# One attention block on one Trainium2 core: another order of a piece's results, exponentials and PV on three engines

## The reference, cut to what matters

```python
# x: (1, 2048, 512); 16 heads, rank 128, rope 64, everything in float32
xn = layernorm(x)
q = (xn @ wq.T).reshape(B, S, 16, 192); q_nope, q_pe = q[..., :128], rope(q[..., 128:])
kv = xn @ wkv_a.T; kv_cache = rmsnorm(kv[..., :128], kv_norm_w); k_pe = rope(kv[..., 128:])
q_lat = einsum('bshd,hdc->bshc', q_nope, wkv_b[:, :128])
scores = (einsum('bshc,btc->bsht', q_lat, kv_cache) + einsum('bshr,btr->bsht', q_pe, k_pe)) * SCALE
attn = softmax(where(causal, scores, -1e30))
out = einsum('bshc,hdc->bshd', einsum('bsht,btc->bshc', attn, kv_cache), wkv_b[:, 128:])
x = x + out.reshape(B, S, 2048) @ wo.T + xn @ ternary(w_ffn).T + bias
```

## Time and profile before

| | |
|---|---|
| three runs | 2119.6, 2119.89, 2128.14 us; median 2119.89 us |
| the profiled execution | 2115.17 us, span 2113.1 us |
| busy share of the span | PE 85%, PE weight loads 72%, VectorE 57%, GpSimd 48%, ScalarE 40% |
| granted TensorE clock over the span | 0.92 |

### The profile page before, as it was taken

One profiled execution on the slowest core, in us unless ns is written; L12 is line 12 of the kernel. 1 busy time (PEld: TensorE's weight loads), 2 busy tenths in 40 slices (PEclk: granted clock), 3 DMA queues, 4 the chain that ended last, 5 costly groups with the idle time before them and its releaser, 6 DMA issues.

```text
span 2113.1 us, 28101 instructions
## 1 busy us (share of the span) xinstructions
PE 1803.1 (85%) x9326; PEld 1523.3 (72%) x9326; DVE 1208.9 (57%) x2801; ACT 853.5 (40%) x1358; POOL 1004.4 (48%) x635
## 2 busy tenths in 40 slices
PE   6997888778989979889888898788898888888885
PEld 5786666657777767777777777677677777777775
DVE  5764566646666655656465555455555555555552
ACT  4552443433444433344444434243443434334342
POOL 4763444434554554454444545344444544445443
PEclk9888899989999999999999999898999989999998
DMA  6992555547656565654444535546455455453544
GB/s 226 356 315 100 147 141 157 162 133 186 169 151 161 148 190 138 168 134 116 119 125 121 136 102 132 158 98 174 112 121 125 104 128 123 114 131 95 127 105 102
DMA packets 127183, 309.11 MB, mean 146 GB/s; under 512 B 29442, under 2 KB 41987, under 8 KB 125508
## 3 DMA queue, kind: packets, MB, share of 16 engines
q1 hardware_dynamic: 117152, 273.20, 48.6%
q10 hardware_dynamic: 9892, 34.18, 5.5%
HBM read 113.28 MB, written 34.60 MB: 70 GB/s over the span
## 4 chain that ended last, share of the span: by engine, by line
PE 28%; issue 20%; POOL 13%; SPq 12%; ACT 8%; DMA 5%; DVE 5%; POOLq 0%; ACTq 0%; DVEq 0%
SPq L986 11%; PE p_score L1101 10%; PE p_out L1121 9%; POOL pT L1367 7%; DMA pT<-turned 5%; PE p_result L1133 4%; DVE turned L1192 3%; ACT pT_h L1286 3%; PE p_lat L1081 3%; ACT probs L1275 3%; POOL qp_l L1356 3%; POOL qp_l L1359 3%; PE p_rot L1081 2%; ACT qp_h L1310 2%; DVE probs L1170 1%
## 5 line engine op out<-in xcount | busy, mean ns | idle before, releaser
L1367 POOL TENSOR_TENSOR pT<-pT,pT_h 128x1024 fp32r<-128x1024 f32 x320 | 684.1, 2164 | 576.4 <-ACT pT_h L1286 574.3
L1170 DVE TENSOR_SCALAR_CACHE_REDUCE probs<-p_score 128x512 f32<-128x512 f32 (+3 forms) x640 | 382.8, 602 | 617.7 <-PE p_score L1101 435.3
L1121 PE MATMUL p_out<-pT_h,V_h 128*128 128x256 f32 (+3 forms) x1024 | 327.9, 320 | 198.0 <-DVE o_l L1219 103.4
L1286 ACT ACTIVATE pT_h<-pT 128x1024 fp32r<-128x1024 f32 x320 | 291.4, 963 | 451.7 <-DMA pT<-turned 296.1
L1275 ACT ACTIVATE probs<-probs,neg_max 128x128 f32<-128x128 f32 (+15 forms) x256 | 307.0, 1199 | 378.9 <-DVE neg_max L1176 376.8
L1121 PEld LDWEIGHTS p_out<-pT_h,V_h 128*128 128x128 f32 x1024 | 213.2, 208 | 235.3 <-DVE o_l L1219 116.1
L1192 DVE STREAM_TRANSPOSE turned<-probs 128x1024 f32<-128x1024 f32 (+7 forms) x384 | 341.5, 915 | 28.2 <-ACT probs L1275 23.4
L1121 PE MATMUL p_out<-pT,V_h 128*128 128x256 f32 (+3 forms) x1024 | 323.0, 315 | 0.0
L1121 PE MATMUL p_out<-pT_h,V_l 128*128 128x256 f32 (+3 forms) x1024 | 321.8, 314 | 0.0
L1101 PE MATMUL p_score<-Kn_h,q_h 128*128 128x512 f32 (+3 forms) x640 | 249.4, 390 | 18.0 <-DVE q_l L1215 18.0
L1101 PE MATMUL p_score<-Kp,qp_h 128*128 128x512 f32 (+3 forms) x640 | 242.6, 379 | 21.3 <-POOL qp_l L1359 20.5
(11 more groups left out here) (135 smaller groups left out, 2390.0 us busy)
## 6 DMA issues: line engine op xcount, KB each, us to landing
pT<-turned SPq DMA_DIRECT2D x512, 128.0 KB, 2.3
Wq<-wq_scr ACTq DMA_DIRECT2D x63, 512.0 KB, 4.5
Wv<-wv_scr SPq DMA_DIRECT2D x63, 512.0 KB, 3.6
pT<-turned SPq DMA_DIRECT2D x256, 112.0 KB, 2.3
pT<-turned SPq DMA_DIRECT2D x256, 96.0 KB, 2.2
pT<-turned SPq DMA_DIRECT2D x256, 80.0 KB, 2.1
pT<-turned SPq DMA_DIRECT2D x256, 64.0 KB, 2.5
Wp<-wp_scr SPq DMA_DIRECT2D x31, 512.0 KB, 4.3
```

Of the source, the lines that this page charges most:

```text
L1121: mm = pe.matmul(out[:, :, cols, :], v[:, t, :], pt[:, :, t - first, rest, :], start=(t == 0 and a == 0), stop=(t == piece_tiles(s) - 1 an ...
L1170: dve.tensor_scalar(probs[row % ROW_RING][:, b * CW:b * CW + width], p_score[n % SCORE_RING][:, 0:width], SCALE, LOWEST, ALU.mult, ALU.max ...
L1286: act.activation(high.rearrange("p r t i q -> p r t (i q)"), low.bitcast(F32).rearrange("p r t i q -> p r t (i q)"), ACT.Copy).then_inc(p_ ...
L1367: pool.tensor_tensor(low.rearrange("p r t i q -> p r t (i q)"), low.bitcast(F32).rearrange("p r t i q -> p r t (i q)"), high.bitcast(F32). ...
```

## The change

Nothing is computed otherwise, and no buffer or instruction is added or removed. Seven things stand elsewhere in the engines' lists:

1. ScalarE: in chunk 3 the three first high copies of a piece move from ahead of the last exponential of slot s + 1 to the start of slot s + 2, behind it (`high_place`); in chunks 0 and 2 they move from unit 0 to unit 1. Within a unit, exponentials now come ahead of the copies of the query and the rotary part.
2. TensorE: PV runs in units 3, 4, 5 and 6 of a slot of chunk 3 (before 1, 3, 5, 7) and in 3, 4, 5 of chunk 2 (before 2, 3, 4) (`value_unit`).
3. The split of PV's result moves in chunk 3 from unit 0 of slot s + 3 to unit 7 of slot s + 2, and in chunk 2 from unit 5 of slot s + 2 to unit 0 of slot s + 3 (`split_place`, which follows `value_unit`).
4. VectorE transposes the last row of the piece before at unit 0, not 1, of each slot from 17 on.
5. The results of an earlier head go in chunk 3 to units 0, 1, 2, 2 (before 2, 3, 4, 5) (`out_unit`).
6. The query projections of chunk 3 begin a unit earlier; in chunks 0 and 3 the query's split is one unit earlier.
7. The rotary part moves: in chunk 0 TensorE makes it ahead of the slot's scores and VectorE does all five rotations at unit 0; in chunk 3 it is one unit later.

```diff
 def value_unit(s, k):
-    return (2 + k, 1 + k, 2 + k, 1 + 2 * k)[phase(s)]
+    return (2 + k, 1 + k, 6 - groups_of(s - 2) + k, 3 + k)[phase(s)]
@@ high_place
     if k < HIGH_RING:
-        return (s + 2, 0) if phase(s + 1) in (0, 2) else (s + 1, units_of(s + 1) - 1)
+        return (s + 1, units_of(s + 1) - 1) if phase(s + 1) == 1 else (s + 2, 0 if phase(s + 1) == 3 else 1)
     return s + 2, value_unit(s + 2, k - HIGH_RING)
@@ out_unit
-    return 2 + i if s % 2 == 0 else i
+    return 0 if s % 2 else (2 + i if phase(s) == 2 else (0, 1, 2, 2)[i])
@@ latent_unit
-    return (it if phase(s) == 2 else 1 + it) if s < SLOTS and closes_head(s) else None
+    return it if s < SLOTS and closes_head(s) else None
@@ query_unit
     if s < 2 * H:
-        return (3, 6)[phase(s)]
-    return (4 if phase(s) == 2 else 5) if s < SLOTS and closes_head(s) else None
+        return (2, 6)[phase(s)]
+    return 4 if s < SLOTS and closes_head(s) else None
 
 def rotate_ops(s, u):
     if phase(s) == 0:
-        return ((), (0, 1, 2), (3, 4), ())[u]
-    return ((0,), (1, 2), (3, 4))[u - 1] if 1 <= u <= 3 else ()
+        return range(5) if u == 0 else ()
+    first = rotary_unit(s) + 1
+    return ((0,), (1, 2), (3, 4))[u - first] if first <= u <= first + 2 else ()
+
+def rotary_unit(s):
+    return 1 if phase(s) == 3 else 0
 
 def rotary_add_unit(s):
-    return (2 if phase(s) == 0 else 4) if opens_head(s) else None
+    return (1, 4, 4, 5)[phase(s)] if opens_head(s) else None
 
 def rotary_high_unit(s):
-    return (3 if phase(s) == 0 else 5) if opens_head(s) else None
+    return (2, 5, 5, 6)[phase(s)] if opens_head(s) else None
@@ TensorE's slot
                 for u in range(units_of(s)):
+                    rotary = u == rotary_unit(s) and opens_head(s) and g % 2 and g + 1 < HEADS
+                    if rotary and s < H:
+                        project_rotary(g + 1)
                     if s < SLOTS:
                         scores(g, unit_of_head(s, u))
-                    if u == 0 and opens_head(s) and g % 2 and g + 1 < HEADS:
+                    if rotary and s >= H:
                         project_rotary(g + 1)
@@ VectorE's slot
-                    if 1 <= s <= SLOTS and u == (1 if s > H else 0):
+                    if 1 <= s <= SLOTS and u == 0:
                         turn_row(head_of(s - 1), first_row(s - 1) + rows_of(s - 1) - 1)
@@ ScalarE's slot
-                    if u == query_unit(s) and g + 1 < HEADS:
-                        high_query(g + 1)
-                        if g + 2 < HEADS:
-                            load_q(g + 2)
                     for old in (s - 3, s - 2):
...
                             if (s, u) == high_place(old, k):
                                 high_group(old, k)
+                    if s < SLOTS and (u + 1) % (chunk_of(g) + 1) == 0 and u + 1 < units_of(s):
+                        exp_row(g, first_row(s) + u // (chunk_of(g) + 1))
+                    if u == query_unit(s) and g + 1 < HEADS:
+                        high_query(g + 1)
+                        if g + 2 < HEADS:
+                            load_q(g + 2)
                     if u == rotary_high_unit(s) and g + 1 < HEADS:
                         high_rotary(g + 1)
-                    if s < SLOTS and (u + 1) % (chunk_of(g) + 1) == 0:
-                        exp_row(g, first_row(s) + u // (chunk_of(g) + 1))
+                if s < SLOTS:
+                    exp_row(g, first_row(s) + rows_of(s) - 1)
```

## The result

| | before | after |
|---|---|---|
| median of four runs | 2119.97 us (2119.6 to 2128.14) | 1905.83 us (1902.1 to 1907.81) |
| profiled execution, its span | 2115.17, 2113.1 us | 1902.1, 1900.0 us |
| granted clock over the span | 0.92 | 0.968 |
| ratio of after to before | | 0.898, 95% 0.8954 to 0.9005 |

The account below looks back on a forecast made before the run. A cycle of exchange, copies, exponential and transposition, not TensorE's work, was taken to pace chunk 3. Gains 95 + 66 + 12 + 21 + 5 - 8 = 191 us gave 1924, and 1929 for the median; forecast 1893 to 1970, range 1885 to 2010.

Parts of the forecast that it names:

- The ring: Chunk 3: exchange, copies, exponential and transposition wait on each other in a cycle of 22.0 us a slot, setting the pace.
- The exchange term: Chunk 3: one exchange takes 13.7 us from its start to its copies, of which 10.07 is issuing.
- The work floor: Chunk 3: TensorE's work at full clock is 70.6 us of the 89.2 us that slots 80 to 83 take.
- Chunk 3: 95 forecast: A four-slot period falls from 89.2 to 75.6 us, 3.4 a slot; 99 over 29 regular slots, taken as 95.
- the 3.0 of new waits: Chunk 3: results waiting for the split and additions add 2.5 us in an even slot, 0.5 with the rotary projection.
- Chunk 2: 66 forecast: Four slots fall from 68.9 to 59.2 us, 2.4 a slot; 68 over 28 slots, taken as 66.
- term for the six slots around the chunk changes, 12 us: The six slots around the chunk changes gain about 2 us each, 12 in all.
- Chunk 1: 21 forecast: An earlier transposition shortens PV's waits in seven slots: 15 us of idle time and 6 of clock gained.
- Chunk 0: 8 lost forecast: The third result waits about 3.4 us in every second slot; idle time even, clock drops in seven slots lose 8 us.
- exchanges slow down in denser traffic: Rival: the same DMAs packed into less time slow the exchanges; 1995 us, up to 2015 with clock falls; chance 0.17.
- The bound of 1995 us: Exchanges 1.9 us later throughout: chunk 2 pays 53 us, chunk 1 pays 13, chunk 3's cover takes it.
- The rival that short waits keep the clock down: Chunks 2 and 3: new waits of 0.5 to 1.2 us hold the clock low, losing 79 us; 2008 us; chance 0.08.

## Why the prediction was right, point by point

- **What bounds chunk 3: right, but one of two bounds.** The ring was taken as 22.0 us a slot from the earlier trace rows. With the copies put back a slot takes 21.0 us and the copies wait for exchanges again. What the prediction did not price is the second bound, PV's early place. With the exchange out of the ring but PV early, a slot still takes 21.4 us in the kernel before and 22.0 in the changed one. The prediction counted both moves as parts of the change, so its sum did not need this.
- **The exchange term: right for the kernel before.** It was sized by one exchange, 13.7 us. From the first issue to the last landing in the trace, the 26 exchanges of pieces 68 to 93 took 11.7 to 15.6 us there, 13.6 on average; with the copies put back and with only PV moved the average is 13.2. The expectation for PV alone kept 13.7, which is about half of its miss of 0.9 us a slot (21.3 for 20.4). Why the average is 0.4 us shorter is open; single exchanges in one profile differ by ten times as much.
- **The work floor: right.** 70.6 us were worked out for a period of four slots; the sum of the four above has PE busy 71.11 at full clock. Before, it was 77.06, so the lower clock cost 5.95 us of busy time, where the guess that three quarters of it were worked gave 6.5.
- **Chunk 3: 95 forecast, 113.5 measured.** The failing terms are the two added on top, "0.9 (in half of the 2.5-us slots the clock falls)" and "1.1 for uneven landings", and half of the 3.0 of new waits. The regular slots run at 1.00, the cover takes uneven landings whole, and the waits are 0.96 + 0.31 and not 2.5 (the 0.5 for `o_l` did not come) and 0.11 and not 0.5. That makes 72.6 for the 75.6, 0.75 a slot, 22 us over 29 slots. Slot 68's wait for the residual and its clock, not foreseen, take some 4 to 5 of it back.
- **Chunk 2: 66 forecast, 80.3 measured.** The wait of results on `o_l` was 1.2 (1.6), in one slot of four as said; again neither a clock drop nor a PV stall came. The period of slots 46 to 49 (1008.0 to 1064.6 us) is 56.6, from 59.2 forecast and 68.9 before; at 3.1 a slot that would be 86 over 28 slots. The **term for the six slots around the chunk changes, 12 us, was wrong**: the results' wait for the residual costs 3.5 us in slot 36 too (none before), and the wait at the end of each chunk stays. It is TensorE's rotary projection for the next chunk waiting for that chunk's `xT`, whose load is issued at 1236.03 and lands 12.3 us later; the projection starts at 1248.40. It is 12.9 us in slot 62 of the changed kernel, where before the projection waited 7.8 us and the PV after it 4.6:

```profile
PE p_rot L1086 <- issue: 12.9, 1, 12.9
```

- **Chunk 1: 21 forecast, 10.9 measured.** The PV stalls fell from 23.2 us in seven to 4.9 in three, more than said, and busy time by 6.4 us for the 6 of clock. What the step left out is an order that the diff shows: exponentials now stand ahead of the rotary copies on ScalarE, so the additions come later and almost every slot has 0.7 to 0.9 us of waiting for `acc`, 13.6 us for 0.5 before. Moving that one copy back removes these waits, which shows the cause; it returned 6 us and not 13, since PV stalls took its place.
- **Chunk 0: 8 lost forecast, 2.7 gained.** The wait on `acc` is there, 3.0 us in every second slot for 3.4. The scores' wait for the rotary low half fell in return, from 19.3 to 15.6 us, and that for the query's low half from 18.0 to 2.5, so idle time stayed about even, as forecast (53.7 and 52.2 us). The clock drop that was to follow in seven slots came in three; in the kernel with late results, whose chunk 0 is the same code, it came in six and the chunk took 265.3 us. So the 2.7 us are not clear of the spread.
- **End: 5 forecast, 5.8 measured.**
- **The sum: its small miss is partly luck.** Chunks 2 and 3 with the chunk changes were forecast at 173 us and gave 193.8, chunk 0 gave 10.7 more than forecast, chunk 1 gave 10.1 less. The last two nearly cancel, and the 12 us for the chunk changes, which did not come, hid more than half of the padding.
- **The rivals.** That exchanges slow down in denser traffic did not happen. The DMA share rose from 0.50 to 0.60, and by the trace the exchanges took 13.4 us on average in chunk 3 (13.6 before) and 12.4 in chunk 2 (13.0 before; pieces 38 to 60). One of chunk 2, 13.7 us from its start to its copies:

```profile
1011.93 4.95 SPq L991 DMA_DIRECT2D pT<-turned  x8
...
1017.60 4.96 SPq L991 DMA_DIRECT2D pT<-turned  x8
...
1025.59 2.96 ACT L1294 ACTIVATE pT_h<-pT 128x1024 fp32r<-128x1024 f32 x3 [0.69 <-DMA pT<-turned]
```

  The Trainium skill's rule that DMAs from all issuing engines share the 16 DMA engines (DMA: Bandwidth & Descriptors, Issuing engines are not separate DMA queues) asked for caution here; at a share of 0.60 the averages show no cost of it. The bound of 1995 us, by which chunk 2 "has no cover", was too dark: a delay of 1.3 to 1.5 us of every exchange of chunks 2 and 3 cost the whole kernel 11 us in the median. The rival that short waits keep the clock down also failed. Waits of 0.3 to 1.2 us in every fourth slot left the clock at 1.00 from 879.0 to 1234.1 us in chunk 2 and from 1371.9 to 1843.6 in chunk 3. The lower level came in four places of these chunks, at waits of 2.2 us (slot 33), 3.5 (slot 36), 12.9 (slot 62, clock 0.72) and 3.5 (slot 68, 0.85); at one of 2.9 us in slot 64 it did not. The Trainium skill (TensorE: Matmul & The Clock Gate, A second HAM failure mode: psum-queue depth-cycling) tells of a kernel in which TensorE is briefly idle between groups of matmuls so often that the clock goes down and up; its section HAM oscillation, which the prediction names, is about long waits for DMAs. With one or two short waits in four slots the trace shows no such change of the clock. What a wait at every group of matmuls would do, no run shows.
- **Not settled:** what brings the PV stalls of chunk 1 when the rotary copy goes first, and why the lower level of the clock comes in three slots of chunk 0 in one profile and six in another. No kernel separated these.

## What to carry to other kernels

Where two engines wait for each other across iterations, add up the ring from its own rows and set it against the busy time of the bounding engine. If the ring is longer, it sets the pace. But look also for the next bound behind it, because an edit that removes one of two bounds may show little: here 15 and 50 us for one each, and 117 for both. After such a cut read the waits again at once. The stall moved from `o_l` to `acc` or to GpSimd's `pT`; its name says what came last, and only the order of work around it says what sets the pace. When a stall is removed, count what the clock gives back as well, which was over a third of the gain in chunks 2 and 3. In chunk 3 padding for clock drops and uneven landings was the larger part of the forecast's error: the waits that remained were about a microsecond, and the landings had cover.

## What the runs showed of the hardware that was not expected

- TensorE kept its full clock through repeated waits of 0.3 to 1.2 us: 1.00 from 879.0 to 1234.1 and from 1371.9 to 1843.6 us after the change. Before, a stall of 1.8 us was followed by the lower level in slot 49, one of 1.5 in slot 81 was not the earlier trace rows, and after the change one of 2.2 us was and one of 2.9 was not. So the length of a single wait does not decide it in this range.
- A DMA issue on SyncE's queue took 0.42 to 0.48 us for a small one (three in 1.25 to 1.44 us) and 0.62 us for one of an exchange (eight in 4.95 us). So the 16 issues, 10.1 to 10.9 us in the exchanges shown, are most of the 11.7 to 15.6 us that an exchange of chunk 3 takes.
